# Attention with float32 splitting: where the product with V and the row sums of the probabilities stand in TensorE's order

## The reference

```python
x = x + attn(layernorm(x))        # (8, 1024, 512)
# attn:
qk = x @ W_qk + b_qk              # q and k interleaved, per head 64
v = (x @ W_v + b_v)
sim = einsum('bihd,bjhd->bhij', q, k) * 64 ** -0.5
o = einsum('bhij,bjhd->bihd', softmax(sim), v)
return (layernorm(o @ W_out + b_out) * gamma + beta + x) * RSQRT2
# then x = x + ffn(layernorm(x)), with three 512 x 512 products and a shift by one token
```

## Time and profile before

| | |
|---|---|
| median of 3 runs | 2723.48 us (2719.68 to 2723.65) |
| the profiled execution | 2721.03 us, its span 2719.2 us |
| TensorE matmuls busy | 2625.8 us, 97% |
| VectorE, ScalarE, GpSimd busy | 60%, 47%, 56% |
| granted TensorE clock, mean | 0.989 of full speed |

### The profile page before, as it was taken

How to read it: one execution, slowest core, us unless ns; L and a number is a source line. 1 busy time by engine, 2 the same in 40 slices (tenths; PEclk the granted TensorE clock), 3 DMA queues, 4 the chain that set the end, 5 groups by cost and what they waited for, 6 DMA issues and landing times. The chain is left out here.

```text
span 2719.2 us, 31997 instructions
## 1 busy us (share of the span) xinstructions
PE 2625.8 (97%) x11376; PEld 1782.0 (66%) x11376; DVE 1631.3 (60%) x2679; ACT 1290.6 (47%) x1833; POOL 1521.1 (56%) x819
## 2 busy tenths in 40 slices
PE   6999999999999999999999999999579999999999
PEld 5655656665565666556556666665358888888887
DVE  7555455456545545654554555455278787878785
ACT  3345346335534634553463455344245555555554
POOL 3576477567647756764775676577323333333333
PEclk9999999999999999999999999999779999999999
DMA  2222122122112212211221221122322222222220
GB/s 97 63 47 51 36 78 53 42 71 55 44 38 75 55 40 71 57 42 48 66 55 40 70 60 39 40 50 79 122 90 99 85 96 89 93 92 89 96 77 32
DMA packets 108410, 178.32 MB, mean 66 GB/s; under 512 B 22401, under 2 KB 22913, under 8 KB 108289
## 3 DMA queue, kind: packets, MB, share of 16 engines
q1 hardware_dynamic: 108288, 176.75, 22.5%
HBM read 92.02 MB, written 50.59 MB: 52 GB/s over the span
## 5 line engine op out<-in xcount | busy, mean ns | idle before, releaser
L417 DVE TENSOR_REDUCE half_max<-ps_max 128x1 f32<-128x512 f32 x1024 | 680.3, 687 | 549.7 <-PE ps_max L780 543.4
L324 POOL TENSOR_TENSOR acc<-acc,probs 128x1024 f32<-128x1024 f32 x384 | 914.0, 2380 | 157.5 <-ACT probs L623 109.2
L623 ACT ACTIVATE probs<-ps_st 128x1024 f32<-128x1024 f32 x512 | 522.0, 1023 | 591.8 <-PE ps_st L801 589.6
L812 PE MATMUL ps_o<-probs,v 128*64 128x512 f32 x2048 | 467.7, 598 | 0.0
L800 PE MATMUL ps_st<-qA,kA 128*128 128x512 f32 x1024 | 415.3, 406 | 13.9 <-DMA qB<-max_row 9.4
L801 PE MATMUL ps_st<-qB,kB 65*128 65x512 f32 x1024 | 408.2, 399 | 0.0
L780 PE MATMUL ps_max<-kA,qA 128*128 128x512 f32 x1024 | 386.8, 416 | 3.7 <-issue 1.4
L320 POOL TENSOR_TENSOR acc<-probs 128x1024 f32<-128x1024 f32 x64 | 152.8, 2387 | 287.6 <-ACT probs L623 287.6
L812 PEld LDWEIGHTS ps_o<-probs,v 128*64 128x64 f32 x2048 | 135.6, 136 | 265.4 <-issue 236.5
L780 PEld LDWEIGHTS ps_max<-kA,qA 128*128 128x128 f32 x1024 | 188.6, 188 | 138.6 <-issue 63.5
L800 PEld LDWEIGHTS ps_st<-qA,kA 128*128 128x128 f32 x1024 | 194.7, 190 | 82.3 <-ACT probs L623 32.7
(11 more groups left out here) (174 smaller groups left out, 4629.6 us busy)
## 6 DMA issues: line engine op xcount, KB each, us to landing
stage<-in_L_attn_x_dram SPq DMA_DIRECT2D x32, 512.0 KB, 5.8
qA<-qA SPq DMA_DIRECT2D x128, 128.0 KB, 2.3
kB<-kA SPq DMA_DIRECT2D x128, 128.0 KB, 2.4
o_hi_scratch<-spare SPq DMA_DIRECT2D x128, 128.0 KB, 2.3
o_lo_scratch<-oT SPq DMA_DIRECT2D x128, 128.0 KB, 2.4
o_hi<-o_hi_scratch SPq DMA_DIRECT2D x16, 1024.0 KB, 5.4
o_lo<-o_lo_scratch SPq DMA_DIRECT2D x16, 1024.0 KB, 7.7
xc<-in_L_attn_x_dram SPq DMA_DIRECT2D x16, 1024.0 KB, 5.2
```

What stands on the lines that cost most here:

```text
L324: pool.tensor_tensor(acc[:, :], acc[:, :], probs[:, j, :], ALU.add).then_inc(acc_done, 1)
L417: dve.tensor_reduce(half_max[:, r, kh:kh + 1], ps_max[(j + 1) % 2][:, :], AX_X, ALU.max).then_inc(max_done, 1)
L623: act.activation(probs[:, j, :], ps_st[j % 2][:, :], ACT.Exp).then_inc(exp_done, 1)
L812: ins = pe.matmul(ps_o[half * DH:(half + 1) * DH, :], v[:, j, hd * DH:(hd + 1) * DH], probs[:, j, half * HALF:(half + 1) * HALF], start=(j ...
```

## The change

In plain heads and at places 6 and 7 the first half of the product with V no longer stands in the middle of its own head: it is issued at the beginning of the next, ahead of the second half, as one burst of 16 pairs. Only place 7 (whose v is overwritten by the next batch) and the last head keep it in the middle; at place 0 the beginning therefore has 8 pairs as before. In plain heads the row sums move from behind the burst to behind 8 of the 12 matmuls of the projection (`sums_now=False`); elsewhere they stay behind the burst. The banks of the row tiles swap: tile 0 writes `ps_max[0]` and waits for the row of maxima, tile 1 `ps_max[1]` and waits for the sums. In plain heads the row and score tiles are interleaved anew. On ScalarE the copy of the sums moves behind the stores of o, but not at place 0, 6 and 7.

```diff
-            bank = ps_misc if t in (4, 5, 6) else ps_max[1] if t in (1, 3) else ps_max[0]
+            bank = ps_misc if t in (4, 5, 6) else ps_max[1] if t in (1, 3, 7) else ps_max[0]
...
# VectorE, reduce_max
-                        dve.tensor_reduce(half_max[:, r, kh:kh + 1], ps_max[(j + 1) % 2][:, :], AX_X,
+                        dve.tensor_reduce(half_max[:, r, kh:kh + 1], ps_max[j % 2][:, :], AX_X,
...
# ScalarE, plain_head (scaling_head alike)
                     if h >= 1:
-                        store_sums(b, h - 1)
+                        if h % HEADS == 0:
+                            store_sums(b, h - 1)
                         store_o(b, h - 1)
                     if h >= 2:
                         store_o_hi(b, h - 2)
+                    if h >= 1 and h % HEADS != 0:
+                        store_sums(b, h - 1)
...
# TensorE, rows
-                            if h >= 2:
-                                pe.wait_ge(sum_copied, 8 * b + h - 1)
-                        if j == 1 and h >= 1:
-                            pe.wait_ge(max_row_done, 8 * b + h)
+                            if h >= 1:
+                                pe.wait_ge(max_row_done, 8 * b + h)
+                        if j == 1 and h >= 2:
+                            pe.wait_ge(sum_copied, 8 * b + h - 1)
...
-                def begin_head(b, h):
+                def begin_head(b, h, sums_now=True):
 
                     if h >= 1:
+                        if h % HEADS != 0:
+                            p_at_v(b, h - 1, 0)
                         p_at_v(b, h - 1, 4)
-                        sum_rows(b, h - 1, 8 * b + h + 1)
+                        if sums_now:
+                            sum_rows(b, h - 1, 8 * b + h + 1)
                     turn_max(b, h)
 
                 def plain_head(b, h, last):
-                    begin_head(b, h)
+                    begin_head(b, h, False)
                     free_of_qk(b, h + 1, 0)
                     project_qk(b, h + 1, 1, 0, 4)
                     rows(b, h + 1, 0, 1)
                     project_qk(b, h + 1, 1, 4, 8)
+                    if h >= 1:
+                        sum_rows(b, h - 1, 8 * b + h + 1)
+                    project_qk(b, h + 1, 1, 8, 12)
                     rows(b, h + 1, 1, 2)
-                    project_qk(b, h + 1, 1, 8, 12)
-                    rows(b, h + 1, 2, 3)
                     scores(b, h, 0, 1)
-                    rows(b, h + 1, 3, 4)
-                    scores(b, h, 1, 3)
-                    rows(b, h + 1, 4, 6)
+                    rows(b, h + 1, 2, 4)
+                    scores(b, h, 1, 2)
+                    rows(b, h + 1, 4, 5)
+                    scores(b, h, 2, 3)
+                    rows(b, h + 1, 5, 6)
                     scores(b, h, 3, 4)
-                    rows(b, h + 1, 6, 8)
+                    rows(b, h + 1, 6, 7)
                     more = not (last and h == HEADS - 2)
                     if more:
                         free_of_qk(b, h + 1, 1)
                         project_qk(b, h + 2, 0, 0, 4)
+                    rows(b, h + 1, 7, 8)
                     scores(b, h, 4, 5)
                     rows(b, h + 1, 8, 10)
                     scores(b, h, 5, 6)
-                    p_at_v(b, h, 0)
-                    rows(b, h + 1, 10, 12)
-                    scores(b, h, 6, 7)
-                    rows(b, h + 1, 12, 13)
+                    rows(b, h + 1, 10, 11)
                     if more:
                         project_qk(b, h + 2, 0, 4, 8)
-                    rows(b, h + 1, 13, 14)
+                    rows(b, h + 1, 11, 12)
+                    scores(b, h, 6, 7)
+                    rows(b, h + 1, 12, 14)
                     scores(b, h, 7, 8)
...
# late_v_head (place 0) and turning_head (place 6), each in the middle
-                    p_at_v(b, h, 0)
...
# early_v_head (place 7)
                     turn_xhat(b + 1, 6, turn_bank(6))
-                    pe.wait_ge(max_row_done, 8 * b + h + 1)
+                    pe.wait_ge(sum_copied, 8 * b + h)
                     turn_xhat(b + 1, 7, turn_bank(7))
```

More of the change, by code:

```diff
@@ L779, in rows @@
                             pe.wait_ge(max_done, 128 * b + 16 * h + j - 1)
-                        pe.matmul(ps_max[(j + 1) % 2][:, :], qA[h % 2][:, r * P:(r + 1) * P],
+                        pe.matmul(ps_max[j % 2][:, :], qA[h % 2][:, r * P:(r + 1) * P],
                                   kA[h % 2][:, kh * HALF:(kh + 1) * HALF], start=True, stop=True).then_inc(rows_done, 1)
```

## The result

The kernel after takes 2727.36 us (median of 22 runs), the one before 2721.68 us (22 runs). Two of the runs after took 2953.18 and 9155.05 us and are left out of the comparison. The ratio of the two is 1.0018, with a 95% interval of 1.0012 to 1.0025: the change costs 0.18%, some 4.9 us (3.3 to 6.8), where the forecast was 3.0. The profiled execution of the kernel after took 2727.23 us, its span is 2725.4 us.

A forecast was written before the change was run, and what follows sets the result against it. TensorE's order of instructions and its small waits bound the kernel. Plain heads +2.5, place 6 +4.9, place 0 and the first head -4.4 gave +3.0 us on a median of 2723.48: 2726.5 us, range 2714 to 2738.

The forecast's parts named there:

- Bursts, nothing in plain heads: Switches into the 64-column shape: joining the V bursts saves 0.33 us, the sums' own switch costs 0.33 in plain heads.
- Row tile 0, -0.25: With the other bank it no longer waits for ScalarE's copy of the sums: -0.25 us in plain heads and place 0.
- Row tiles 4 and 5, +0.87: In plain heads they wait for VectorE's low part of k and reduce 3, so score tile 3 comes 0.87 us late.
- The other waits, -0.80: Plain head's old waits go: 0.25 us at row tile 0, 0.31 for the exponential, 0.24 for VectorE at row tiles.
- Place 6, +0.70: Without the middle burst row tiles 7 and 8 wait for VectorE: -0.33 + 1.23 - 0.25 + 0.05 us, seven heads.
- Place 0, -0.58: One burst fewer, -0.33 us, and no wait at row tile 0, -0.25, in seven heads.
- place 7, 0,: Keeps its middle burst; a transposition's new wait for the sums' copy is covered by the wait for maxima: 0.
- Rival B: Sums' copy, moved behind the stores of o on ScalarE, stops row tile 1: 2735 to 2747 us, chance 0.17.
- Rival C: VectorE runs the low parts ahead of reduce 2, so row tiles 4 and 5 aren't stopped: 2696 us, chance 0.14.

The follow-up runs named there:

- two row tiles ahead: Kernel after, in plain heads row tile 2 ahead of score tile 0 and a third of the next projection ahead of row tile 5: 2710.16 us.
- the mended order: As two row tiles ahead, with row tiles behind score tile 5 spread, place 6's middle burst back, its sums behind four projection matmuls: 2696.83 us.
- the low parts first: Kernel after with VectorE doing the low parts of the projection's second half ahead of reduce 2: 2744.0 us, 1.0078 of the kernel before.

## Why the forecast held, and where its size was off

**The size.** The forecast change was +3.0, the measured one +4.9, and the heads alone show +4.2. The time came closer, 2726.5 against 2727.36, and that is luck: the median of three runs that I started from is 1.8 above the one of 22.

**The bound.** That TensorE's order and its waits set the time held in every kernel: what a plain head gained or lost is found in the starts of TensorE, and the times follow the plain heads. But another engine comes close: in the shorter heads with the sums in the first burst GpSimd stops TensorE 42 times.

**Bursts, nothing in plain heads.** -0.33 for the joined burst and +0.33 for the sums: the second is shown directly (0.34 by putting the sums back), the first by the kernels with bursts apart (25.67 against 25.33) and by place 0 of the joined burst alone (36.94 against 37.30).

**Row tile 0, -0.25.** Shown by the swap alone, 0.25 a head.

**Row tiles 4 and 5, +0.87.** The chain was as worked out. Reduce 2 to the low part of k are 0.73 (917.43 to 918.16; I took 0.72, the lower bound was 0.60). By the section "Two Vector instructions with no wait between them" of the page "VectorE: DVE Perf Modes" in the Trainium skill, an instruction in another quadrant is held until the earlier one is through; the trace agrees, for the reduce takes 0.69 and ends at 918.12, 0.04 before the low part of k starts. From the low part of k to reduce 3 are 1.45 (I had 1.46). Score tile 3 is at 16.20, worked out 16.16. The kernel with two row tiles ahead shows that this wait is what eats the gain: without it, and with the new wait of 0.24, the head is at 25.56, and at 25.33 when that is mended too.

**The other waits, -0.80,** went as forecast: no row tile but 4 and 5 is late. A plain head is +0.10, not +0.06; the 0.04 times 41 is 1.6 us, the term of the sum that was mis-sized most. It isn't one wait: the projection behind the sums is at 10.33 (I had 10.30) and row tile 2 at 12.52 (12.49), 0.01 more comes by score tile 3, and 0.02 in the steps behind it.

**Place 6, +0.70.** It was +0.74: 1.29 lost at row tiles 7 and 8 where I had 1.23. Of the 0.05 for GpSimd at most 0.03 was taken: the sums start at 6.92, and what follows them starts 0.99 later, before 0.96. Putting the middle burst back took the loss away.

**Place 0, -0.58,** was -0.62, **place 7, 0,** was -0.05.

**Rival B** is refuted. The copy of the sums starts at 10.44 of the head and ends at 11.04 (I had 10.4 and 10.98), row tile 1 isn't late. The margin is 0.32, of which 0.22 is needed, so it did not take much.

**Rival C** is refuted by the run that gave it its condition.

**What I left out:** the first 75 us. Without them the change adds 4.2 us in the heads, -0.3 in the first head's burst and -0.4 at the end, together 3.5. The slower clock adds 2.7 to the profiled span. The other profile of the kernel after has 3.3 of it, the one with the sums in the burst 3.3, those with place 6's burst put back and with the mended order 2.7 and 2.6, and the two with the bursts apart 3.6 (sums late) and 3.0. The kernel before has none, and 0.1 to 0.4 at most have the swap alone, the joined burst alone, the two row tiles ahead and the low parts first, the last of which has the whole of TensorE's new order. So the new order doesn't bring it by itself. In all twelve profiles the slow stretch at 58 us goes with the moment at which the clock first rose: where the last of the early starts 0.43 apart is at 31.1 to 31.5 (five profiles) it is missing, where it is at 32.0 to 34.1 (seven) it is there. This moment isn't the program's alone, for the kernel after has it at 33.3 in one profile and at 32.0 in the other. The eleven runs of the kernel with place 6's burst put back lie in two groups, 2719.3 to 2720.0 and 2722.0 to 2723.5, and the profiled one, with the loss, is in the upper. Both point to chance in each execution, but no kernel was profiled with the loss and without it, so whether it can belong to a program stays open: the runs of the kernel before lie from 2719.0 to 2724.4 us and those of the kernel after from 2724.6 to 2729.0, a spread in both that is larger than this loss. The interval of the ratio, 3.3 to 6.8 us, holds the sum with the loss and without it.

## What to carry to other kernels

When an engine is full, ask of every long block in its order what other engine catches up behind it: the middle burst cost a switch of 0.33 and gave VectorE 3.8 us, and joining it to the other gained nothing until the row tiles were spread anew. Work out the distance, in steps, between each instruction and the one that frees its bank, with the full queue of the engine in between: six steps (1.40 us) were enough behind one reduce and not behind one reduce and a low part. Try the parts of a change alone: here one part gained 0.47%, another lost 0.5%, and the sum said "nothing".

## What was new about the hardware

A wait that lies under the overlap of two matmul records leaves no bracket, and its end can be foretold: the instruction behind a waiting row tile started 0.40 (920.28 to 920.68) and 0.38 us (918.92 to 919.30) after VectorE's end. One switch into the 64-column shape and back cost 0.33 to 0.34 us whether it framed 8 pairs of the product with V or 2 pairs of sums. And behind the same idle times of TensorE (1.35 and 1.29 us) the granted clock was 0.50 for some 3.2 us in the kernel after (starts 0.43 apart from 58.64 to 61.20) and 1.00 in the kernel before; the profiles differ in when the clock had first risen, 2.2 us later in the kernel after.
